# Four blocks of expert 0 moved into the end of the tile stage, and the adds made straight into the output

## The chip, the cores and the metric

The kernel runs on one core of one Trainium2 chip. The metric is the device time of the program in microseconds (us). Engines are called TensorE (PE in rows; PEld is its weight load), VectorE (DVE), ScalarE (ACT), GpSimd (POOL) and SyncE (SP, which here only issues transfers and waits). A "q" behind an engine's name means its queue.

## The reference

Cross attention of 2 x 1024 tokens of width 256 to 77 context rows with 16 heads, and then a feed-forward layer that is a mixture of 8 experts, of which each token uses the two with the highest logits:

```python
x = x + xattn(layernorm(x), ctx, ctx, mask, Wq, bq, Wk, bk, Wv, bv, Wo, bo)
x = x + ffn(layernorm(x), ln1_g, ln1_b, attn_w, ln2_g, ln2_b, gate_w, gate_proj, up_proj, down_proj)

def ffn(x, ...):
    h = x + (layernorm(x) * ln1_g + ln1_b) @ attn_w.T
    t = layernorm(h) * ln2_g + ln2_b
    logits = t @ gate_w.T                                 # 2048 x 8
    top_vals, top_idx = top_k(logits, 2)
    rw = softmax(top_vals)
    for e in range(8):
        g, u = t @ gate_proj[e].T, t @ up_proj[e].T       # 256 -> 1024
        out += comb[:, e:e+1] * ((silu(g) * u) @ down_proj[e].T)   # 1024 -> 256
    return h + out
```

Everything is 32-bit float.

## The kernel before

**Tile stage.** The 2048 tokens are 16 tiles of 128, batch 0 and 1 in turn. A software pipeline runs over them: in step `it` each engine does the stages LN1, XT, QK, PV, PROJ, LN2, MIX, LIST and SCATTER (lags 0 to 8) of the tiles it, it-1, ..., it-8. So steps 16 to 23 drain the pipeline, with fewer stages each. Each engine has its own instruction order, written out in a function `tiles(it)`; semaphores join them. On ScalarE step `it` ends with the exponentials of tile it-2 (`p_sb`, L646), and the next begins with `qT` (L611), which the score products (L1100) wait for. GpSimd computes the inverse roots of the norms (L495 to L498), scatters each tile's list entries (L517) and adds the residual (L523). SyncE stores each tile's normalized rows to `z2_rows` and its residual to `acc_rows` (`store`, L417).

LIST finds each token's two experts, and its place in each of their lists by two small products with the tokens before it (L1118, L1119). SCATTER writes (token, weight) into the lists in device memory, 2048 places for each expert.

**Seam.** When all tiles are listed, TensorE adds up the counts (L1162), and VectorE computes the tables on one partition (L910 to L956): how many blocks of 128 rows each expert has, which list row each block starts at (`row_tab`, released by `row_done`), which of three weight buffers it uses, and in which block the next expert's weights are to be split (`tab_done`). ScalarE, VectorE and GpSimd split expert 0's weights into a high and a low part there (L661, L656, L531, L966 to L968), since each expert product is made as three products of rounded pieces (L1168 to L1170).

**Expert stage.** A pipeline over 36 usual blocks (`USUAL_BLOCKS`; up to three more if present): GpSimd fetches the block's list (L553), gathers its rows (L560), TensorE transposes them (L1208, here called the block transposes), ScalarE and VectorE make the pieces `tb_hi` and `tb_lo`; TensorE computes gate and up in two halves (24 products of 512 columns in all, 6 for each half product), ScalarE silu, VectorE `act`; TensorE transposes act (L1199), the pieces `aT_hi` and `aT_lo` are made, then down is 24 products of 256 columns; VectorE weights the result (L979), GpSimd adds it to the rows in `acc_rows` by an accumulating indirect transfer (L570). SyncE loads the weights of experts 2 to 7 in four parts each (L439), as buffers come free. When all adds are in, SyncE copies `acc_rows` to the output (L447).

```python
            def experts_(it, only=None):                      # TensorE, L1182
                a, b, c = back(it, 0), back(it, 1), back(it, 2)
                # gate and up of b (half 0), act transposes of c, gate and up of b (half 1),
                # block transposes of a, down of c
```

## Time and profile before

| | us |
|---|---|
| median of 3 runs | 621.02 (617.53 to 622.01) |
| the profiled execution | 620.13 |
| its span | 618.6 |
| mean granted clock of TensorE | 0.932 of full speed |

The profile shows one execution, in microseconds from the start of its span. Busy time of an engine: TensorE 527.6 us (85%), VectorE 345.9 (56%), ScalarE 281.4 (45%), GpSimd 287.2 (46%). The granted clock is the share of TensorE's full clock that it was given. A timeline row gives start, length, engine, line, operation, output and inputs, and in brackets how long the engine had been idle before, and what released it. Several equal instructions in a row are merged (x2). The ends of matmuls are modelled: the pace is read from the distance of their starts.

### The profile page before, as it was taken

How to read it: one execution, taken by the hardware profiler on the slowest of the kernel's cores; microseconds unless marked ns; L12 is line 12 of the kernel's file. 1: busy time of each engine (PE TensorE's matmuls, PEld its weight loads, DVE VectorE, ACT ScalarE, POOL GpSimd, SP SyncE). 2: the span in 40 equal slices, each digit the busy share in tenths (PEclk: the TensorE clock that was granted, in tenths of full speed). 3: DMA queues.
4: the chain of work that ended last, by engine and by line, in shares of the span. 5: the costliest groups of instructions: out<-in, count | busy, mean ns of one | idle time of the engine just before them, and what ended most of it. 6: DMA issues, size and time to landing. Idle time of an engine off the chain costs nothing.

```text
span 618.6 us, 13662 instructions
## 1 busy us (share of the span) xinstructions
PE 527.6 (85%) x3197; PEld 452.7 (73%) x3198; DVE 345.9 (56%) x876; ACT 281.4 (45%) x701; POOL 287.2 (46%) x374
## 2 busy tenths in 40 slices
PE   2579999999997513899999998999999999999960
PEld 1357788888886302788888887888888888888850
DVE  1846788788876474466434345836536534365330
ACT  1177878787874141534323325434335323353210
POOL 4321436455545455357633416756554644345120
PEclk9779999999998555999999999899999999999995
DMA  8870010101010044011312375171262222612123
GB/s 217 217 314 0 19 36 18 35 17 34 17 35 27 27 86 161 10 28 27 44 26 34 77 211 178 17 200 55 43 187 59 34 43 28 179 55 34 17 23 143
DMA packets 27088, 46.57 MB, mean 75 GB/s; under 512 B 9718, under 2 KB 22544, under 8 KB 26768
## 3 DMA queue, kind: packets, MB, share of 16 engines
q1 hardware_dynamic: 15312, 35.77, 17.8%
q0 software_dynamic: 9088, 9.52, 9.7%
q10 hardware_dynamic: 2656, 0.91, 0.9%
q8 instruction: 13, 0.21, 0.2%
q14 instruction: 19, 0.16, 0.1%
HBM read 36.67 MB, written 11.61 MB: 78 GB/s over the span
## 4 chain that ended last, share of the span: by engine, by line
PE 65%; ACT 12%; DMA 7%; DVE 4%; issue 3%; POOL 1%; ACTq 0%; POOLq 0%; SPq 0%; DVEq 0%
PE psum L1168 15%; PE psum L1169 15%; PE psum L1170 15%; ACT p_sb L646 9%; PE psum L1100 6%; DMA w_raw<-in_experts 6%; PE psum L1199 4%; PE psum L1048 4%; PE psum L1043 2%; PE psum L1208 1%; ACT qT L611 1%; ACT uT L635 1%; PE psum L1055 1%; ACT rows L640 1%; PE psum L1064 1%
## 5 line engine op out<-in xcount | busy, mean ns | idle before, releaser
L1168 PE MATMUL psum<-w_hi,tb_hi 128*128 x288 | 117.9, 409 | 5.1 <-DVE tb_lo L1004 4.2
L1169 PE MATMUL psum<-w_lo,tb_hi 128*128 x288 | 113.7, 395 | 0.0
L1170 PE MATMUL psum<-w_hi,tb_lo 128*128 x288 | 113.7, 395 | 0.0
L1168 PE MATMUL psum<-w_hi,aT_hi 128*128 x288 | 85.0, 295 | 4.3 <-DVE aT_lo L992 4.3
L1169 PE MATMUL psum<-w_lo,aT_hi 128*128 x288 | 82.1, 285 | 0.0
L1170 PE MATMUL psum<-w_hi,aT_lo 128*128 x288 | 82.1, 285 | 0.0
L992 DVE TENSOR_TENSOR aT_lo<-psum,aT_hi 128x512 fp32r<-128x512 f32 x72 | 46.4, 685 | 63.0 <-ACT aT_hi L678 63.0
L674 ACT ACTIVATE silu<-psum 128x512 f32<-128x512 f32 x36 | 21.6, 600 | 117.4 <-PE psum L1170 117.4
L570 POOL DMA_INDIRECT acc_rows<-o_sb,add_at x36 | 58.6, 1629 | 34.1 <-POOL add_at L568 32.9
L998 DVE TENSOR_TENSOR act<-psum,silu 128x512 f32<-128x512 f32 x72 | 49.3, 686 | 33.8 <-PE psum L1170 28.5
L1168 PEld LDWEIGHTS psum<-w_hi,tb_hi 128*128 128x128 f32 x288 | 54.9, 191 | 16.9 <-issue 7.3
L646 ACT ACTIVATE p_sb<-s_sb,s_negmax 128x77 f32<-128x77 f32 x256 | 65.5, 348 | 1.1 <-DVE s_negmax L811 1.1
L560 POOL DMA_INDIRECT rows<-z_rows,gather_at x36 | 47.8, 1327 | 34.9 <-POOL gather_at L558 27.0
L1170 PEld LDWEIGHTS psum<-w_hi,tb_lo 128*128 128x128 f32 x288 | 54.7, 190 | 12.0
L1169 PEld LDWEIGHTS psum<-w_lo,tb_hi 128*128 128x128 f32 x288 | 54.9, 191 | 9.3
L1168 PEld LDWEIGHTS psum<-w_hi,aT_hi 128*128 128x128 f32 x288 | 55.6, 193 | 4.8 <-issue 4.8
L678 ACT ACTIVATE aT_hi<-psum 128x512 fp32r<-128x512 f32 x72 | 39.1, 595 | 43.6 <-PE psum L1199 43.6
L1169 PEld LDWEIGHTS psum<-w_lo,aT_hi 128*128 128x128 f32 x288 | 55.9, 194 | 0.0
L1170 PEld LDWEIGHTS psum<-w_hi,aT_lo 128*128 128x128 f32 x288 | 55.8, 194 | 0.0
L373 POOL TENSOR_TENSOR w_lo<-w_raw,w_hi (+1 forms) x8 | 34.6, 4325 | 45.2 <-DVE w_hi L988 45.2
L979 DVE TENSOR_SCALAR o_sb<-psum,blk 128x256 f32<-128x256 f32 x36 | 17.4, 482 | 65.8 <-PE psum L1170 30.6
L496 POOL TENSOR_SCALAR var_eps<-mv 128x1 f32<-128x1 f32 x48 | 11.6, 241 | 89.6 <-DVE mv L713 48.2
(170 smaller groups left out, 1029.5 us busy)
## 6 DMA issues: line engine op xcount, KB each, us to landing
w_raw<-in_experts SPq DMA_DIRECT2D x24, 768.0 KB, 4.4
w_raw<-in_experts SPq DMA_DIRECT2D x2, 3072.0 KB, 14.0
x_sb<-in_x SPq DMA_DIRECT2D x8, 256.0 KB, 5.8
z_rows<-rows SPq DMA_DIRECT2D x16, 128.0 KB, 1.7
acc_rows<-x_sb SPq DMA_DIRECT2D x16, 128.0 KB
ceil_f<-in_mask ACTq DMA_DIRECT2D x2, 308.0 KB, 11.6
blk<-lists POOLq DMA_DIRECT2D x36, 1.0 KB
rows<-z_rows,gather_at POOLq DMA_INDIRECT x36, 2.9
```

Source lines behind the costliest of these rows:

```text
L373: return engine.tensor_tensor(weights(w_lo, slot, at, cols), weights(w_raw, slot, at, cols), weights(w_hi, slot, at, cols).bitcast(F32), A ...
L560: nc.gpsimd.indirect_dma_start(zg[:, b[1], :], None, z2_rows, bass.IndirectOffsetOnAxis(ap=gather_at[:, b[1], :], axis=0), bounds_check=TO ...
L570: nc.gpsimd.indirect_dma_start(acc_rows, bass.IndirectOffsetOnAxis(ap=add_at[:, c.par, :], axis=0), y[:, c.par, :], None, bounds_check=TOK ...
L646: last = nc.scalar.activation(p_sb[:, t2[1], h * KEYS:(h + 1) * KEYS], s_sb[:, t2[1], h * KEYS:(h + 1) * KEYS], ACT.Exp, bias=s_negmax[:, ...
L678: nc.scalar.activation(aT_hi[:, c.par, 4 * half:4 * half + 4, :], bank[4 + half], ACT.Copy).then_inc(aTh_done, 1)
L992: nc.vector.tensor_tensor(aT_lo[:, c.par, 4 * half:4 * half + 4, :], bank[4 + half].rearrange("p (i t) -> p i t", i=4), aT_hi[:, c.par, 4 ...
L998: nc.vector.tensor_tensor(act[:, b.par, half * 512:half * 512 + 512], bank[1 + 2 * half], silu[:, half, :], ALU.mult).then_inc(act_done, 1)
L1048: done = nc.tensor.matmul(dst, rows_T[:, k, :], w[:, k, :], start=k == 0, stop=k == KD - 1)
L1100: last = nc.tensor.matmul(bank[g][:, (h0 - g * BANK_HEADS) * KEYS:(h1 - g * BANK_HEADS) * KEYS], qT[:, par, m, :], k_diag[:, par, m, h0 - ...
L1168: nc.tensor.matmul(dst, hi, weights(w_hi, slot, at, cols), start=first, stop=False)
L1169: nc.tensor.matmul(dst, hi, weights(w_lo, slot, at, cols), start=False, stop=False)
L1170: return nc.tensor.matmul(dst, lo, weights(w_hi, slot, at, cols), start=False, stop=last)
```

## The change

Rows 0 to 511 of expert 0's list are known once the first nine tiles are listed (if those tiles give at least 512; else the rest is left as padding and later tokens start at row 512). The change does these four blocks early, and starts the tables' count for expert 0 at row 512:

- SyncE fetches their list rows after tile 10's store. GpSimd waits in step 17 for them, for the stores, and for the last exponentials (the gathered rows, `ze`, lie over `p_sb`), and gathers block 0; blocks 1, 2 and 3 follow in steps 18, 20 and 21.
- Expert 0's weights are split in the tile stage: a quarter on ScalarE in steps 4 to 7, its low part on VectorE in steps 5 to 8. The buffers of the tile stage are laid out anew for that.
- The work of blocks 0 and 1 is written into steps 18 to 21 of TensorE, ScalarE and VectorE; the rest of block 1, and blocks 2 and 3, are written between VectorE's table operations. The late blocks follow as before, 32 of them, with their tables from index 0.
- Expert 1's split is fixed to block 3, and expert 2's load waits for the transposes of block 5.
- From tile 13 on GpSimd computes the router's exponential, as a power of e, instead of ScalarE.
- Rank products of the tiles behind 11 go to another bank of PSUM.
- `acc_rows` is the output itself, so rows are in the output's order (batch first), and the copy at the end is gone. All of `z2_rows` is filled with zeros in the prologue.

```diff
+EARLY, EARLY_TILES = 4, 9
+LIST_ROWS = EARLY * P + EXPERTS * TOKENS + SPARE * P
...
-        acc_rows = nc.dram_tensor("acc_rows", (TOKENS + P, D), F32).ap()
+        acc_rows = out
...
-            sp.dma_start(z2_rows[TOKENS:TOKENS + P, :], zeros[:, :]).then_inc(pad_out, 16)
+            sp.dma_start(z2_rows.rearrange("(c p) d -> p c d", p=P), zeros[:, :].unsqueeze(1).to_broadcast([P, TILES + 1, D])).then_inc(pad_out, 16)
...
-            pipeline(sp, store, TILES, 0, 0)
+            sp.wait_ge(pad_out, 32)
+            pipeline(sp, store, EARLY_TILES + 1, 0, 0)
+            store(Step((EARLY_TILES + 1) // 2, (EARLY_TILES + 1) % 2, 2))
+
+            for par in range(2):
+                sp.wait_ge(listed[par], 16 * TOPK * len(range(par, EARLY_TILES, 2)))
+            for j in range(EARLY):
+                sp.dma_start(blk[:, j], lists[j * P:(j + 1) * P, :]).then_inc(blk_early, 16)
+            for t in range(EARLY_TILES + 2, TILES):
+                store(Step(t // 2, t % 2, 2))
 
...
                 if e == 2:
                     sp.wait_ge(acc_out, 16 * TILES)
+                    sp.wait_ge(tb_ps, EARLY + 2)
...
             sp.wait_ge(added, every)
-            for b in range(BATCH):
-                sp.dma_start(out_tiles[:, b], acc_tiles[:, b]).then_inc(out_done, 16)
-            sp.wait_ge(out_done, 16 * BATCH)
+            sp.sem_inc(out_done, 1)
...
+                if within(t7, TILES) and isinstance(number(t7), int) and number(t7) >= SILU_TILES:
+
+                    pool.wait_ge(gap_done, number(t7) + 1)
+                    nc.gpsimd.tensor_tensor(e2[:, t7[1], :], base_e[:, :], gap[:, t7[1], :], ALU.pow).then_inc(e2p_done, 1)
...
+                if at_step(it, 17):
+                    for par in range(2):
+                        pool.wait_ge(z2_out[par], 16 * len(range(par, EARLY_TILES, 2)))
+                    pool.wait_ge(pad_out, 32)
+                    pool.wait_ge(p_done, PT_ROUNDS * TILES)
+                    pool.wait_ge(blk_early, 16 * EARLY)
+                    nc.gpsimd.tensor_copy(gather_at[:, :, :], blk[:, 0:EARLY, 0:1]).then_inc(ate_done, 1)
+                    wait_apart(pool, ate_done, 1, pool_met)
+                    gather_early(0)
+                if at_step(it, 18):
+                    gather_early(1)
+                if at_step(it, 20):
+                    gather_early(2)
+                if at_step(it, 21):
+                    gather_early(3)
+
...
+                if isinstance(number(it), int) and 4 <= number(it) < 8:
+
+                    at, cols = split_columns(number(it) - 4)
+                    act_e.wait_ge(w_in[0], 16)
+                    nc.scalar.activation(weights(w_hi, 0, at, cols), weights(w_raw, 0, at, cols), ACT.Copy).then_inc(hi_first, 1)
+
+                if at_step(it, 18):
+                    tb_out(block_(0))
+                if at_step(it, 19):
+                    tb_out(block_(1))
+                    silu_out(block_(0), 0)
+                    silu_out(block_(0), 1)
+                if at_step(it, 20):
+                    aT_out(block_(0), 0)
+                    silu_out(block_(1), 0)
+                if at_step(it, 21):
+                    aT_out(block_(0), 1)
...
+                if isinstance(number(it), int) and 5 <= number(it) < 9:
+
+                    at, cols = split_columns(number(it) - 5)
+                    dve.wait_ge(hi_first, number(it) - 4)
+                    nc.vector.tensor_tensor(weights(w_lo, 0, at, cols), weights(w_raw, 0, at, cols),
+                                            weights(w_hi, 0, at, cols).bitcast(F32), ALU.subtract).then_inc(lo_first, 1)
+
+                if at_step(it, 19):
+                    tb_pieces(block_(0))
+                if at_step(it, 20):
+                    act_out(block_(0), 0)
+                    act_out(block_(0), 1)
+                    tb_pieces(block_(1))
+                if at_step(it, 21):
+                    aT_rest(block_(0), 0)
+                    aT_rest(block_(0), 1)
+                    act_out(block_(1), 0)
...
-            step(nc.vector.tensor_copy(cnt[:, :], bank[0][0:1, 0:EXPERTS]))
+            step(nc.vector.tensor_tensor(cnt[:, :], bank[0][0:1, 0:EXPERTS], taken[:, :], ALU.add))
+            tb_pieces(block_(2))
+            weighted(block_(0))
...
-            step(nc.vector.tensor_scalar(row_tab[:, :], r_of[:, :], float(P), None, ALU.mult))
+            step(nc.vector.tensor_scalar(row_tab[:, :], r_of[:, :], float(P), float(EARLY * P), ALU.mult, ALU.add))
             dve.sem_inc(row_done, 1)
+
+            act_out(block_(1), 1)
+            for half in range(2):
+                aT_rest(block_(1), half)
+            act_out(block_(2), 0)
...
+            act_out(block_(2), 1)
+            tb_pieces(block_(3))
...
-            down_leftovers(nc.vector, dve, 0, 1, GU_COLS, DN_COLS // 2)
-            leftovers(0, 1, 0)
-            leftovers(0, 1, 1)
...
+                if at_step(it, 20):
+                    up_(block_(0), 1)
+                if at_step(it, 21):
+                    aT_(block_(0), 1)
...
+                if at_step(it, 18):
+                    tb_(block_(0))
+                if at_step(it, 19):
+                    pe.wait_ge(place_done, 13)
+                    tb_(block_(1))
+                    gate_(block_(0), 0)
+                    up_(block_(0), 0)
+                    gate_(block_(0), 1)
+                if at_step(it, 20):
+                    aT_(block_(0), 0)
+                    gate_(block_(1), 0)
+                    up_(block_(1), 0)
+                if at_step(it, 21):
+                    down_(block_(0), 0)
...
+            down_(block_(0), 1)
+            tb_(block_(2))
+            gate_(block_(1), 1)
+            up_(block_(1), 1)
...
+            for i in range(EARLY - 1, EARLY + 1):
+                experts_(block_(i))
+            pe.wait_ge(tab_done, 1)
+            pipeline(pe, experts_, USUAL_BLOCKS, 2, 2 * GATHERS, GATHERS, EARLY + 1)
```

## Rows read from the trace of the kernel before

**Rows 1.** page, forty slices of the span: TensorE's granted clock, in tenths

```profile
PEclk9779999999998555999999999899999999999995
```

**Rows 2.** table of stretches: stretch, length, busy us by engine, clock, DMA share, GB/s

```profile
60.00:120.00 60.00, 57.33 (x390) 48.64 (x389) 47.75 (x175) 49.22 (x168) 28.44 (x55) 1.00 0.08 25
210.00:240.00 30.00, 4.92 (x19) 3.38 (x19) 20.30 (x73) 7.18 (x9) 15.37 (x17) 0.50 0.43 100
```

**Rows 3.** timeline of TensorE: drain, seam, block transposes of blocks 0, 4, 35

```profile
202.65 2.08 PE L1048 MATMUL psum<-aw,uT 128*128 128x256 f32 x4 [0.24 <-ACT uT L635]
...
220.41 0.19 PE L1118 MATMUL psum<-chosen,below 128*128 128x8 bf16 x1 [1.58 <-DVE chosen L788]
...
240.38 0.66 PE L1208 MATMUL psum<-ident,rows 128*128 128x128 f32 x2 [19.51 <-DMA rows<-z_rows,gather_at]
...
278.92 0.38 PE L1208 MATMUL psum<-ident,rows 128*128 128x128 f32 x2
...
580.75 0.38 PE L1208 MATMUL psum<-ident,rows 128*128 128x128 f32 x2
```

**Rows 4.** timeline, end of the span: last add, then the output copy

```profile
600.54 1.58 POOL L570 DMA_INDIRECT acc_rows<-o_sb,add_at  x1 [1.21 <-issue]
605.58 1.62 SPq L447 DMA_DIRECT2D out_x<-acc_rows  x2
```

**Rows 5.** timeline of ScalarE: last exponentials; conversion of weights

```profile
184.19 4.10 ACT L646 ACTIVATE p_sb<-s_sb,s_negmax 128x77 f32<-128x77 f32 x16
...
223.90 3.69 ACT L656 ACTIVATE w_hi<-w_raw 128x2048 fp32r<-128x2048 f32 x2
```

**Rows 6.** chain that ended last, tile stage: start, us, what

```profile
165.88 2.84 ACT p_sb L646 x11
168.72 0.52 ACT qT L611 x2
```

**Rows 7.** timeline of GpSimd: tile 13's root, last scatter, first list fetch

```profile
185.97 0.19 POOL L495 TENSOR_SCALAR var_eps<-mv 128x1 f32<-128x1 f32 x1 [3.91 <-DVE mv L713]
...
223.54 1.18 POOL L517 DMA_INDIRECT lists<-pair,pos  x1 [0.30 <-issue]
...
231.02 0.62 POOL L553 DMA_DIRECT2D blk<-lists  x1 [3.92 <-issue]
```

**Rows 8.** page, DMA issues: out<-in, count, size, median us to landing

```profile
w_raw<-in_experts SPq DMA_DIRECT2D x24, 768.0 KB, 4.4
...
rows<-z_rows,gather_at POOLq DMA_INDIRECT x36, 2.9
```

**Rows 9.** page, costliest groups: VectorE's act operations, busy, mean ns of one

```profile
L998 DVE TENSOR_TENSOR act<-psum,silu 128x512 f32<-128x512 f32 x72 | 49.3, 686 | 33.8 <-PE psum L1170 28.5
```

**Rows 10.** timelines of VectorE and GpSimd: tables and leftover pass

```profile
221.48 0.28 DVE L912 TENSOR_TENSOR passed_n<-cnt,over 1x128 f32<-1x128 f32 x1
...
224.92 2.25 DVE L925 SCALAR_TENSOR_TENSOR r_of<-e_of,steps 1x40 f32<-1x40 f32 x1
...
227.42 0.17 DVE L927 TENSOR_SCALAR row_tab<-r_of 1x40 int32<-1x40 f32 x1
...
224.75 2.36 POOL L373 TENSOR_TENSOR w_lo<-w_raw,w_hi 128x1024 fp32r<-128x1024 f32 x1
```

**Rows 11.** timeline of TensorE: products and act transposes behind the seam

```profile
243.02 0.79 PE L1168 MATMUL psum<-w_hi,tb_hi 128*128 x1 [1.98 <-DVE tb_lo L1004]
...
246.59 0.63 PE L1170 MATMUL psum<-w_hi,tb_lo 128*128 x1
247.02 0.63 PE L1168 MATMUL psum<-w_hi,tb_hi 128*128 x1
...
248.24 0.40 PE L1168 MATMUL psum<-w_hi,tb_hi 128*128 x1
248.48 0.40 PE L1169 MATMUL psum<-w_lo,tb_hi 128*128 x1
...
256.23 1.04 PE L1199 MATMUL psum<-ident,act 128*128 128x128 f32 x8
```

More of the change, by code:

```diff
@@ L667, in experts_ @@
                 has = member(only)
-                if has(c):
+                if has(c) and not early(c):
                     splits = entry(act_e, splits_tab, c, 0, 1)
@@ new lines, in up_, with aT_ @@
+            def up_(b, half, slot=0):
+                n = number(b)
+                if early(b) and n == 0 and half == 1:
+                    pe.wait_ge(pT_done, PT_ROUNDS * TILES)
+                if early(b) and n == 1 and half == 1:
+                    pe.wait_ge(topi_done, TILES)
+                wait_count(pe, act_done, 2 * n - 1 + half)
+                half_product(b, slot, half, 1).then_inc(u_ps, 1)
+            def aT_(c, half):
+                n = number(c)
+                pe.wait_ge(act_done, 2 * n + half + 1)
+                if early(c) and n == 0 and half == 0:
+                    pe.wait_ge(act_done, 2)
+                if early(c) and n == 0 and half == 1:
+                    pe.wait_ge(x1_done, TILES)
+                if early(c) and n == 1 and half == 1:
+                    pe.wait_ge(y_done, 1)
+                wait_count(pe, aTl_done, 2 * n - 1 + half)
+                for i in range(4):
+                    at = half * 512 + i * P
+                    last = nc.tensor.transpose(bank[aT_bank(c, half)][:, i * P:(i + 1) * P], act[:, c.par, at:at + P], ident[:, :])
+                last.then_inc(aT_ps, 1)
@@ new lines, in tb_ @@
+            def tb_(a):
+                n = number(a)
+                if early(a) and n == 0:
+                    pe.wait_ge(q_done, KD * TILES)
+                if early(a) and n == 2:
+                    pe.wait_ge(place_done, TILES)
+                pe.wait_ge(zg_in[a[1]], 16 * (a[0] + 1))
+                wait_count(pe, tb_done, 2 * n)
+                for k in range(KD):
+                    last = nc.tensor.transpose(bank[6][:, k * P:(k + 1) * P], gathered(a)[:, k * P:(k + 1) * P], ident[:, :])
+                last.then_inc(tb_ps, 1)
@@ new lines, in down_ @@
+            def down_(c, half, slot=0):
+                n = number(c)
+                if half == 0:
+                    if early(c) and n == 0:
+                        pe.wait_ge(h_done, TILES)
+                    if early(c) and n == 1:
+                        pe.wait_ge(aTl_done, 2)
+                    wait_count(pe, y_done, n)
+                for i in range(half * IC // 2, (half + 1) * IC // 2):
+                    if i % 4 == 0:
+                        pe.wait_ge(aTl_done, 2 * n + i // 4 + 1)
+                    last = three_products(bank[y_bank(c)][:, 0:D], aT_hi[:, c.par, i, :], aT_lo[:, c.par, i, :], slot,
+                                          GU_COLS + i * D, D, i == 0, i == IC - 1)
+                if half == 1:
+                    last.then_inc(y_ps, 1)
```

345 lines of the change are left out of this document (217 added, 128 removed).

## The prediction

> **What bounds the kernel now.** I read the granted clock in the page's forty slices first [rows 1]: full nearly everywhere, but behind a third of the span it falls to its lower level (0.5 of full speed, 1.2 GHz). The table of stretches says what TensorE does there [rows 2]: in the tile stage it is busy 57.33 of 60 us, from 210 to 240 us only 4.92 of 30. The TensorE timeline of the seam [rows 3] says what the hole is. The last tile's rank product starts at 220.41. The next work is the first block's transpose at 240.38, after 19.51 us of waiting for the gathered rows; in between VectorE builds the tables and GpSimd fetches lists and rows. From then on the pace is TensorE's own: the block transposes (one pair for each of 36 blocks) start at 278.92 for block 4 and at 580.75 for block 35, 301.83/31 = 9.74 us a block. After the last block an add and then a copy of the whole output remain [rows 4]: the last add is issued at 600.54, the copy at 605.58, and the span ends at 618.6. So there are three costs to look at: the hole, 36 blocks, 13.0 us of copy.
>
> **Does the early work replace other work, or come on top?** A block is 128 list rows. From the reference's inputs I counted the routing: expert 0 gets 1279 rows, 749 of them in the first nine tiles (512 are needed), and all experts together need 36 blocks. With 512 rows of expert 0 taken off, 767 are left, 6 blocks instead of 10. So 4 early + 32 later = 36: no padding and no additional block.
>
> **Removed: the output copy.** From 605.58 to the span's end at 618.6: **-13.0 us** [rows 4]. The adds now go into the output itself; each was an add in device memory before too, so I price them alike.
>
> **Added in the tile stage.** ScalarE converts expert 0's weights in four pieces of 1536 columns at steps 4 to 7. Two pieces of 2048 took 3.69 us [rows 5], 1.84 each; three quarters, with a small fixed part, is 1.43 us. What would hide it? The chain of work in the tile stage [rows 6] goes from the exponentials on ScalarE to qT on ScalarE at once (168.72), and from there to the score products. The piece stands between the exponentials and qT, so nothing hides it: 4 x 1.43 = **+5.7 us** (0 if the chain has slack that the rows don't show). VectorE's four leftover pieces come at steps 5 to 8. No row of mine has VectorE at this; ScalarE's pace would make it 1.4 us, GpSimd's (2.36 us for 1024 columns, [rows 10]) 3.5; I take 1.7, nearer the faster one, as VectorE's act operations on 512 columns take 0.69 even out of PSUM [rows 9]. VectorE is busy 47.75 of 60 us in the tile stage [rows 2], which leaves 2 us of each step (about 10.3 us), and three of the four following steps are themselves longer by 1.43. I take these pieces at 0, up to 1.7 each if that cover is gone. The list base has one more small operation and a wait on VectorE in the prologue: +0.3. The zero fill writes seventeen copies of 128 KB instead of one, ahead of the first two experts' 6 MB. It lies beside the tiles' compute, since the first weights are wanted only at step 4; 0, up to 1 us on the loads issued just before it. Sum: S = **+6.0**.
>
> **The drain, step by step** (times as in the profile before, S left out). GpSimd at step 17 now waits for the last exponentials, which end at 184.19 + 4.10 = 188.29 [rows 5], because the gather's target lies over their buffer. Then a small copy, about 1.2 us to the indirect issue, and 1.1 us to issue. Queued behind this is the inverse root of tile 13, which ran at 185.97 [rows 7] and now starts near 190.7: **+4.7**. VectorE's z and o_sb wait for it, and TensorE behind them. I add 0.5 for TensorE's slower clock after that idle: +5.2. Gathered rows land 2.9 us after issue [rows 8], near 192.5, before step 18's end, so the gather itself is hidden.
> Step 19's last product on TensorE ended at 202.65 + 2.08 = 204.7 [rows 3]; now 209.9. Products of 512 columns follow each other every 0.43 us at the lower clock and every 0.23 to 0.24 at the higher [rows 11]. A half gate or up product is 6 of them: 2.6 or 1.4 us. The 8 act transposes of a block take 1.0 [rows 11]. What is left of a block's 9.74 us after four half products (5.6) and the transposes (1.0, 0.2) is the down product, 2.9.
> - Transposes of block 1 (0.4), one half product at the lower clock (2.6), two at the higher (2.8): 215.7.
> - Step 20 took about 4.6 of the 15.7 us from step 19's end to the last rank product [rows 3]; now with a half product (1.4) but mostly at the higher clock, which halves the rest: 3.6, to 219.3.
> - Transposes of act and two half products (3.3) to 222.6, just when the next tile's chosen experts come (some 3.4 us after step 20's last product, again out of those 15.7).
> - VectorE now has three block operations of 0.69 us [rows 9] before the last tile's maximum; the last rank product starts at about 227.25 instead of 220.41: **+6.85**.
> - Pair, count, pieces of block 2 and the weighting of block 0: the tables' second operation starts at 231.25 (was 221.48). From it to the end of the row table was 227.59 - 221.48 = 6.1 us. But one operation of 40 elements took 2.25 us beside GpSimd's 2.36 us leftover pass [rows 10]; the next operation of the same size, the row table's own, takes 0.17 to 0.19, and that pass is gone: 4.05, to 235.3.
> - Meanwhile TensorE does the rest of block 1 and half of block 2 and waits for act of block 1, which VectorE makes behind the row table: 236.05.
> - Transposes, two half products, block 3's transposes, down of block 1: 6.4, to 242.4. Four half products of block 3 (5.6) and act transposes (1.0): block 4's transposes start at **249.0**.
> They started at 278.92: **-29.9 us**. Four blocks at 9.74 are 39.0 us; 9 us of it are lost in the seam. The last list scatter ends near 232; before, the first list fetch came 7.5 us after the last scatter's issue (223.54 to 231.02) [rows 7], beside expert 2's weights. Even with that delay block 4's rows are there near 247, so the gather isn't the bound, by 2 us. Expert 2's load now starts only with block 5's transposes, but is wanted three blocks later (29 us) and its four parts of 4.4 us take 18 [rows 8]: hidden. Behind block 4 all switches of experts fall on the same block numbers as before, so 31 blocks and the end cost what they cost.
> **Where clock and page speak against it.** In the seam the clock fell after the idle time and came back only after about 5 us of dense products (243.0 to 248.2) [rows 11]. The new seam has work in small bursts with waits between. I add **+2.5** for one more stretch at the lower clock.
> The Trainium skill, page "TensorE: Matmul & The Clock Gate", section "HAM oscillation — how this bites in real kernels", says that short bursts of matmuls between waits throttle TensorE again each time, so the bursts keep running at half clock. The trace agrees so far as the clock fell in the drain; whether bursts of 3 to 6 us do it no row shows. It is the first rival below.
>
> **Sum** against the profiled execution's 620.1 us: 620.1 - 13.0 - 29.9 + 6.0 + 2.5 = 585.7, so **586 us**. That execution lies 0.9 under the median of 621.0, less than I can resolve.
>
> **Rivals.**
> 1. *The clock stays at the lower level in the bursts.* For: the clock of 0.5 from 210 to 240 us [rows 1, 2]. Against: from 210 us on TensorE would be dense. Price: the half products on the path to block 4, about 12 that I took at the higher clock, at 1.2 us more each, plus down (2.9) and transposes (some 2): +19. In place of my 2.5: 586 + 17 = **603 us**. If only up to the row table: 594.
> 2. *The tile stage absorbs the pieces, or the GpSimd wait is shorter.* ScalarE was busy 49.22 of 60 us of that stage [rows 2], so a wait could close. Then up to 5.7 + 2.5 less: **578 us**. Against: the chain, where each link follows the other at once [rows 6].
> 3. *Slower than before: the adds into the output set the pace.* An add took 605.4 - 600.54 = 4.9 us from issue to landing, and each next add waits for it; with 1.4 us of preparation it fits in 9.74 us. If adds into the output buffer took over 8.3 us, every microsecond more would cost 36. Slower than 627 us needs 627 - 586 = 41 us, so 9.5 us an add. Against: the copy wrote 2 MB there in 13 us without trouble [rows 4]. **630 us** at 9.6.
> 4. *The change doesn't do what it says*: were block 2 or 3's act held by the tables, early blocks would wait as the first block did, and only the copy and a part would be won: 620.1 - 13.0 + 6.0 = **613 us**.
>
> **How the numbers follow.** Forecast 0.70; rival 1 0.14 (0.06 of it at 600 or more); rival 2 0.09 (0.03 under 577); rival 3 0.02; rival 4 0.05. Range 577 to 600: beyond it lie 0.06 + 0.03 + 0.02 + 0.05 and a few hundredths for what I overlooked. One per cent, about what a measurement here can tell from no change, is 6.2 us: faster 0.95, same 0.02, slower 0.03.
>
> **What would show it.** Right: the block transposes at equal spacing, block 4's starting near 249 + 6 + 2.5 = 257 us; no SyncE copy at the end; the tile steps 4 to 7 longer by 1.4 us; tile 13's inverse root on GpSimd right behind the first gather; the small table operation at 0.2 us. Wrong: a TensorE wait over 5 us in the table stage, the first later block waiting for its gathered rows, a wait at the switch to expert 2, adds over 8 us, or a clock of 0.5 through the early blocks.

## The result, and the profile after

| | before | after |
|---|---|---|
| median of 4 runs, us | 621.51 (617.53 to 622.77) | 588.82 (588.05 to 592.96) |
| profiled execution, us | 620.1 | 589.26 |
| its span, us | 618.6 | 587.7 |
| last exponentials of the tile stage end | 188.29 | 192.90 |
| block 4's transposes start | 278.92 | 255.27 |
| last add issued | 600.54 | 576.18 |

The changed kernel takes 0.9494 of the time before, with a 95% interval of 0.9441 to 0.9548. That is 32.7 us less. The forecast was 586 (577 to 600), so it held, 2.8 us too low. One of its terms, the output copy, was wrong by 6.5 us, though, and misses of the other terms hid about half of that. So the closeness is partly luck.

The seam first. This is the TensorE timeline of the kernel after, from the end of the tile stage to the first block after the tables. The columns are as in [rows 3].

```profile
197.63 0.69 PE L1241 MATMUL psum<-ident,o_sb 128*128 128x128 f32 x2 [4.51 <-DVE o_sb L900]
...
207.29 2.19 PE L1262 MATMUL psum<-v_chunks,pT 128*128 128x34 f32 x10
209.28 0.67 PE L1445 MATMUL psum<-ident,ze 128*128 128x128 f32 x2
...
216.45 1.13 PE L1246 MATMUL psum<-aw,uT 128*128 128x256 f32 x4 [0.49 <-ACT uT L734]
217.42 0.38 PE L1445 MATMUL psum<-ident,ze 128*128 128x128 f32 x2
217.56 0.48 PE L1383 MATMUL psum<-w_hi,tb_hi 128*128 128x512 f32 x1
...
233.12 0.18 PE L1322 MATMUL psum<-chosen,below 128*128 128x8 bf16 x1 [0.74 <-DVE chosen L924]
...
245.79 0.38 PE L1445 MATMUL psum<-ident,ze 128*128 128x128 f32 x2
255.27 0.38 PE L1445 MATMUL psum<-ident,rows 128*128 128x128 f32 x2
264.73 0.38 PE L1445 MATMUL psum<-ident,rows 128*128 128x128 f32 x2
```

The last tile's rank product (L1322) starts at 233.12. Behind it there is no longer a hole of 19.51 us [rows 3]: the early blocks' work runs on, and block 4's transposes, the first out of `rows` instead of `ze`, start at 255.27. The one long wait left is the first line, 4.51 us, and it ends with VectorE's o_sb. VectorE itself waited 4.93 us for a root from GpSimd (`rstd`) just before; its row, and then GpSimd's timeline:

```profile
196.82 0.41 DVE L859 TENSOR_SCALAR z<-x_sb,mv,rstd 128x256 f32<-128x256 f32 x1 [4.93 <-POOL rstd L567]
...
193.17 0.19 POOL L611 COPY gather_at<-blk 128x4 int32<-128x4 int32 x1 [6.42 <-ACT p_sb L745]
194.34 1.09 POOL L600 DMA_INDIRECT ze<-z_rows,gather_at  x1 [0.97 <-POOL gather_at L611]
195.50 0.18 POOL L564 TENSOR_SCALAR var_eps<-mv 128x1 f32<-128x1 f32 x1
...
237.43 0.97 POOL L590 DMA_INDIRECT lists<-pair,pos  x1 [0.30 <-issue]
242.76 0.61 POOL L650 DMA_DIRECT2D blk<-lists  x1 [4.36 <-issue]
```

GpSimd waits for the last exponentials (ACT p_sb), makes the gather's indices, issues the gather, and only then reaches tile 13's inverse root at 195.50. In the table of stretches of the same kernel (stretch, length, busy us of PE, PEld, DVE, ACT and POOL with counts, granted clock, DMA share, GB/s) the clock is at its lower level right behind that wait and back at full from 220 us on:

```profile
190.00:200.00 10.00, 3.87 (x27) 2.92 (x26) 4.24 (x21) 4.33 (x16) 4.99 (x9) 0.75 0.08 24
200.00:210.00 10.00, 9.95 (x40) 8.73 (x38) 3.74 (x14) 2.00 (x6) 4.10 (x8) 0.50 0.23 29
210.00:220.00 10.00, 7.53 (x33) 5.99 (x34) 7.36 (x33) 5.02 (x12) 4.77 (x8) 0.72 0.09 28
220.00:230.00 10.00, 9.36 (x53) 7.35 (x51) 6.84 (x36) 4.58 (x11) 7.24 (x10) 1.00 0.20 54
230.00:260.00 30.00, 27.74 (x169) 24.27 (x170) 21.32 (x74) 8.16 (x16) 17.00 (x22) 1.00 0.17 32
```

Two small things that were to be seen are there. The table operation of 40 elements, 2.25 us in [rows 10], takes 0.19 us now:

```profile
240.96 0.19 DVE L1124 SCALAR_TENSOR_TENSOR r_of<-e_of,steps 1x40 f32<-1x40 f32 x1
```

And the end. This is the last add in the GpSimd timeline of the kernel after:

```profile
576.18 1.57 POOL L667 DMA_INDIRECT out_x<-o_sb,add_at  x1 [0.87 <-POOL add_at L665]
```

This is the view of its line 152, where each engine leaves the program (queue, operation, count: shortest, median and longest ns, first and last start):

```profile
L152 SPq DRAIN  x1: 7/7/7, 580.9 to 580.9; - x1
L152 POOLq DRAIN  x1: 5265/5265/5265, 581.7 to 581.7; - x1
L152 PEldq DRAIN  x1: 73/73/73, 587.4 to 587.4; - x1
```

And this, with the same columns, is the view of its line 393, the test of whether a block behind the usual ones is present:

```profile
L393 PEldq COMPARE_BRANCH  x7: 210/1381/2810, 574.0 to 584.7; - x7
```

A DRAIN is here the last thing that an engine does before the semaphores of the common end. SyncE is done at 580.9, 4.7 us behind the last add's issue, and that is where I had the end of the kernel. But GpSimd's DRAIN runs until 587.0, and TensorE's queue is busy until 587.4 with branches over seven absent blocks. From the last add's issue to the end of the span it is 11.5 us; the forecast had left 5.0 (605.58 - 600.54).

### The profile page after: what moved, and what is told of

It reads as the page before. It is cut to its first block, busy times and chain, and to the rows that moved or that the text cites. A ratio compares the mean times of both kernels' runs of the same rounds, so it can differ in the third digit from the quotient of the medians.

```text
span 587.7 us, 13275 instructions
## 1 busy us (share of the span) xinstructions
PE 523.3 (89%) x3198; PEld 450.5 (77%) x3199; DVE 345.3 (59%) x882; ACT 281.3 (48%) x699; POOL 283.1 (48%) x371
## 3 DMA queue, kind: packets, MB, share of 16 engines
q0 software_dynamic: 8960, 9.51, 10.2%
## 4 chain that ended last, share of the span: by engine, by line
PE 64%; ACT 13%; DVE 6%; DMA 5%; issue 4%; POOL 1%; SPq 0%; ACTq 0%; POOLq 0%; DVEq 0%
PE psum L1383 15%; PE psum L1384 14%; PE psum L1385 14%; ACT p_sb L745 9%; PE psum L1298 6%; DMA w_raw<-in_experts 4%; PE psum L1432 4%; PE psum L1246 4%; PE psum L1241 2%; ACT uT L734 1%; PE psum L1445 1%; ACT qT L710 1%; PE psum L1262 1%; PE psum L1253 1%; ACT rows L739 1%
## 5 line engine op out<-in xcount | busy, mean ns | idle before, releaser
L1383 PE MATMUL psum<-w_hi,tb_hi 128*128 (+1 forms) x288 | 116.8, 405 | 2.7 <-DVE tb_lo L1025 1.7
L1385 PE MATMUL psum<-w_hi,tb_lo 128*128 (+1 forms) x288 | 112.6, 391 | 0.0
L1384 PE MATMUL psum<-w_lo,tb_hi 128*128 (+1 forms) x288 | 112.6, 391 | 0.0
L779 ACT ACTIVATE silu<-psum 128x512 f32<-128x512 f32 x72 | 43.1, 599 | 132.7 <-PE psum L1385 124.9
L1383 PE MATMUL psum<-w_hi,aT_hi 128*128 (+1 forms) x288 | 84.6, 294 | 4.1 <-DVE aT_lo L1036 4.1
L1384 PE MATMUL psum<-w_lo,aT_hi 128*128 (+1 forms) x288 | 81.5, 283 | 0.0
L1385 PE MATMUL psum<-w_hi,aT_lo 128*128 (+1 forms) x288 | 81.4, 283 | 0.0
L667 POOL DMA_INDIRECT out_x<-o_sb,add_at x36 | 59.6, 1656 | 34.2 <-POOL add_at L665 31.8
L1383 PEld LDWEIGHTS psum<-w_hi,tb_hi 128*128 128x128 f32 x288 | 54.2, 188 | 13.3 <-issue 4.1
L1031 DVE TENSOR_TENSOR act<-psum,silu 128x512 f32<-128x512 f32 x72 | 49.4, 687 | 24.9 <-PE psum L1385 18.1
L657 POOL DMA_INDIRECT rows<-z_rows,gather_at x32 | 41.9, 1308 | 30.8 <-POOL gather_at L655 24.2
L1298 PE MATMUL psum<-k_diag,qT 128*128 128x308 f32 (+2 forms) x128 | 40.1, 459 | 15.2 <-ACT qT L710 9.8
L1043 DVE TENSOR_SCALAR o_sb<-psum,blk 128x256 f32<-128x256 f32 x36 | 17.4, 482 | 60.4 <-PE psum L1385 28.9
## 6 DMA issues: line engine op xcount, KB each, us to landing
ceil_f<-in_mask ACTq DMA_DIRECT2D x2, 308.0 KB, 11.5
```

What stands on the lines that cost most here:

```text
L657: nc.gpsimd.indirect_dma_start(zg[:, b[1], :], None, z2_rows, bass.IndirectOffsetOnAxis(ap=gather_at[:, b[1], :], axis=0), bounds_check=TO ...
L667: nc.gpsimd.indirect_dma_start(acc_rows, bass.IndirectOffsetOnAxis(ap=add_at[:, c.par, :], axis=0), y[:, c.par, :], None, bounds_check=TOK ...
L779: nc.scalar.activation(silu[:, half, :], bank[half_banks(b, half)[0]], ACT.Silu).then_inc(silu_done, 1)
L1031: nc.vector.tensor_tensor(act[:, b.par, half * 512:half * 512 + 512], bank[half_banks(b, half)[1]], silu[:, half, :], ALU.mult).then_inc(a ...
L1298: last = nc.tensor.matmul(bank[g][:, (h0 - g * BANK_HEADS) * KEYS:(h1 - g * BANK_HEADS) * KEYS], qT[:, par, m, :], k_diag[:, par, m, h0 - ...
L1383: nc.tensor.matmul(dst, hi, weights(w_hi, slot, at, cols), start=first, stop=False)
```

## The experiments

The question for the end: is the time behind the last add that of the engines' own closing work, which the copy had covered? For the tile stage: what do the pieces cost, and on which engine? For the drain: what do GpSimd's wait and the clock cost? Each kernel below is the changed one with one edit, unless it says otherwise; each ratio is to runs of the kernel before that were taken beside it (medians 618.8 to 621.7). "Not to be told apart by the times" means that the 95% intervals of two ratios overlap widely; the profiles show one execution each.

**Copy put back** (accumulate in a buffer of its own, copy at the end):

```
-        acc_rows = out
+        acc_rows = nc.dram_tensor("acc_rows", (TOKENS + P, D), F32).ap()
...
-            sp.sem_inc(out_done, 1)
+            for b in range(BATCH):
+                sp.dma_start(out[b * SEQ:(b + 1) * SEQ, :], acc_rows[b * SEQ:(b + 1) * SEQ, :]).then_inc(out_done, 16)
+            sp.wait_ge(out_done, 16 * BATCH)
```

> The changed kernel with its own accumulation buffer and the output copy put back at the end; all else as changed. Theory A (the copy used to cover the engines' own way to the end of the program, 6.6 us of it): the copy takes 13.0 us from its issue, which again lies 4.9 us behind the last add's issue, so the span ends 17.9 us behind the last add's issue instead of 11.5, and the time is 6.4 us longer, 595.2 us. Theory B (the copy's 13.0 us were all gained, and the 6.6 us that are missing lie elsewhere, in slower adds into the output): 13.0 longer, 601.8 us, or if the adds become quicker again, something between; the distance from the last add's issue to the copy's issue would then be well under 4.9 us.

Measured 593.3 (592.27 to 595.81), ratio 0.9548 (0.9514 to 0.9581): about 4.5 us more than the changed kernel, not 13. The copy, now of contiguous rows, is issued at 584.30, and SyncE's DRAIN is at 592.9, so this copy took 8.6 us where the one before took 12.7 (605.58 to 618.3). And it isn't what ends the profiled execution of 594.2 us; TensorE's DRAIN is, behind branches of up to 5.06 us beside the copy:

```profile
L152 PEldq DRAIN  x1: 73/73/73, 593.9 to 593.9; - x1
```

Why those branches were longer, and whether the order of the rows made the copy shorter, isn't shown. So this run alone doesn't price the old copy. The next one does.

**The kernel before without its copy** (list and rows in batch order, so that the sums can go into the output):

```
-        acc_rows = nc.dram_tensor("acc_rows", (TOKENS + P, D), F32).ap()
+        acc_rows = out
...
-            for b in range(BATCH):
-                sp.dma_start(out_tiles[:, b], acc_tiles[:, b]).then_inc(out_done, 16)
-            sp.wait_ge(out_done, 16 * BATCH)
+            sp.sem_inc(out_done, 1)
```

> The kernel before with only this part of the change: the adds go straight into the output, rows in the output's order, no copy at the end. My prediction's term was -13.0 us: 608.5 us. Theory A: in the kernel before TensorE's queue was done at 601.9 us and GpSimd's drain at 610.1, against the span's end at 618.6, so only 8 to 8.5 us are gained: 613.2 us; with a drain as long as in the changed kernel (5.3 us from 602.5) up to 10.8: 610.7. Theory B (slow adds into the output): under 7 us gained, and adds longer than before.

Measured 612.72 (610.22 to 614.29), ratio 0.9852 (0.9813 to 0.9892), so 9.0 us less than the 621.69 beside it, clear of noise (the interval gives 7 to 12). Its last add is issued at 603.98 and the span ends at 612.6, 8.6 us behind. This is its GpSimd's closing DRAIN:

```profile
L140 POOLq DRAIN  x1: 6497/6497/6497, 605.9 to 605.9; - x1
```

and this the same in the kernel before, under the copy of [rows 4]:

```profile
L140 POOLq DRAIN  x1: 7635/7635/7635, 602.5 to 602.5; - x1
```

Without a copy the span ends with GpSimd (605.9 + 6.5 = 612.4). In the kernel before GpSimd was busy until 610.1 and nobody saw it, as the copy ran to 618.3. So at most 8 or 9 us could be won there.

**Three tests instead of seven at the end**, and **tests nested**, so that the first absent block skips all others:

```
-            for j in range(USUAL_BLOCKS, EARLY + BLOCKS):
+            for j in range(USUAL_BLOCKS, BLOCKS):
```
```
-            for j in range(USUAL_BLOCKS, EARLY + BLOCKS):
+            def behind(j):
+                if j == EARLY + BLOCKS:
+                    return
                 with eng.If(eng.value_load(present_tab[0:1, j - EARLY:j - EARLY + 1], min_val=0, max_val=1)):
...
+                    behind(j + 1)
+            behind(USUAL_BLOCKS)
```

> The changed kernel with three tests for absent blocks at the end instead of seven (of what is computed nothing changes for these inputs; lists of more than 39 blocks would lose some). Theory A1 (TensorE's queue, which walks over the seven absent blocks until 587.4 us, ends the program): TensorE is done near 580, and GpSimd's drain, which ended at 587.0 in the changed kernel, becomes the end; GpSimd has four tests of 0.78 us less ahead of its drain, so between 0.4 and 3.5 us faster, I take 2.5: 586.3 us. Theory A2 (GpSimd's drain ends a fixed time, about 9.2 us, behind the last add's issue whatever stands ahead of it): 0.4 us faster, 588.4. Theory B (slow adds): no change.

> The changed kernel with the tests for absent blocks nested, each inside the one before, so that one test is made when no block is present and the code of all seven is jumped over at once; nothing is left out. Theory A1: as with three tests or a little better, 585 to 586.5 us. Theory A2: 588.4. If a far jump costs as much as several near ones (the branches of TensorE took 0.2 to 2.8 us each), then not better than three tests.

Three tests: 588.18 (586.03 to 590.59), ratio 0.9484 (0.9439 to 0.9529), not to be told apart from the changed kernel by the times. In the profile the last add to the end of the span is 9.5 us, where it was 11.5. Nested: 585.57 (584.06 to 588.46), ratio 0.9441 (0.9396 to 0.9486), 3.2 us less by the medians with intervals that still overlap, and 9.2 us from the last add to the end. The closing of both queues in the nested kernel:

```profile
L152 PEldq DRAIN  x1: 73/73/73, 575.1 to 575.1; - x1
...
L152 POOLq DRAIN  x1: 5897/5897/5897, 576.9 to 576.9; - x1
```

TensorE is through 1.3 us behind the issue of the last add (573.82), where it was 11.2 in the kernel after, and GpSimd's DRAIN alone sets the end (576.9 + 5.9 = 582.8, of 583.0). One branch of 3.36 us is left on TensorE, and it ends at 575.0, before GpSimd's DRAIN starts. GpSimd's tests cost less than their own length: in the seven kernels that make one or three of them its DRAIN takes 6.5 to 7.6 us where it starts about 2 us behind the last add's issue, and 5.8 to 5.9 where it starts about 3 behind, and it ends 8.4 to 9.6 behind; in the seven kernels with seven tests it takes 5.27 and ends 10.7 to 10.8 behind. In five of the kernels below that keep the seven tests the span ends 12.0 to 13.0 us behind the last add, always with TensorE's DRAIN, while GpSimd's ends before: there TensorE's walk over the absent blocks decides.

**ScalarE's pieces twice**, each of the four written a second time by the same operation behind the first:

```
                     nc.scalar.activation(weights(w_hi, 0, at, cols), weights(w_raw, 0, at, cols), ACT.Copy).then_inc(hi_first, 1)
+                    act_e.wait_ge(hi_first, 2 * (number(it) - 4) + 1)
+                    nc.scalar.activation(weights(w_hi, 0, at, cols), weights(w_raw, 0, at, cols), ACT.Copy).then_inc(hi_first, 1)
```

> The changed kernel with each of ScalarE's four conversions of expert 0's weights (tile steps 4 to 7) made twice. Theory A (they stand on the chain from the exponentials to the score products, nothing covers them): a second time adds 4 x 1.4 to 1.5 us: 588.8 + 5.8 = 594.6 us, steps 4 to 7 are 13.1 us long. Rival B (part was covered by waits): under 3 us more.

Measured 602.69 (602.05 to 603.69), ratio 0.9724 (0.9677 to 0.977): 13.9 us more, over twice what was expected. The tile stage alone grew by 12.7 (here and below from the third tile's score products to the last exponentials). First the chain in the kernel after (ScalarE and TensorE timelines):

```profile
61.45 4.09 ACT L745 ACTIVATE p_sb<-s_sb,s_negmax 128x77 f32<-128x77 f32 x16
65.44 1.48 ACT L753 ACTIVATE w_hi<-w_raw 128x1536 fp32r<-128x1536 f32 x1
66.82 0.61 ACT L710 ACTIVATE qT<-psum,bq_scaled 128x128 f32<-128x128 f32 x2
...
67.48 2.34 PE L1298 MATMUL psum<-k_diag,qT 128*128 128x462 f32 x8 [1.72 <-ACT qT L710]
```

then a step of the doubled one:

```profile
67.70 1.47 ACT L753 ACTIVATE w_hi<-w_raw 128x1536 fp32r<-128x1536 f32 x1
69.20 1.48 ACT L755 ACTIVATE w_hi<-w_raw 128x1536 fp32r<-128x1536 f32 x1
70.59 0.61 ACT L710 ACTIVATE qT<-psum,bq_scaled 128x128 f32<-128x128 f32 x2
...
71.25 4.47 PE L1300 MATMUL psum<-k_diag,qT 128*128 128x462 f32 x8 [3.24 <-ACT qT L710]
```

and two stretches of its tile stage:

```profile
60.00:90.00 30.00, 23.07 (x126) 18.48 (x125) 19.06 (x46) 22.09 (x59) 7.06 (x16) 0.83 0.05 18
90.00:120.00 30.00, 26.41 (x162) 21.63 (x162) 23.54 (x76) 22.33 (x67) 11.61 (x20) 0.88 0.06 19
```

The piece lies between exponentials and qT, as forecast, and each copy adds 1.4 to 1.5 us to TensorE's wait (0.35 without a piece, 1.72 with one, 3.24 with two). The rest goes with the clock: in the changed kernel it was 1.00 in these stretches, and here it is 0.83 and 0.88. From these mean clocks some 17 of the 60 us ran at the lower level, an estimate, which can cost up to 8.7 us; 6.8 were to be explained. The same eight score products take 4.47 us instead of 2.34 when the clock has fallen in that wait. The longer wait isn't needed for it: the profiled execution with the copy put back has the same in a milder form, though its tile stage and its waits of 1.72 us are those of the changed kernel: score products of 4.02 us, two steps of 13.3 us, 3.2 us more in the stage.

**VectorE's work twice** (one more pass of 1536 columns ahead of each leftover):

```
                     dve.wait_ge(hi_first, number(it) - 4)
+                    nc.vector.tensor_tensor(weights(w_hi, 0, at, cols), weights(w_hi, 0, at, cols).bitcast(F32),
+                                            weights(w_hi, 0, at, cols).bitcast(F32), ALU.max).then_inc(hi_again, 1)
+                    dve.wait_ge(hi_again, number(it) - 4)
```

> The changed kernel with one more VectorE pass of 1536 columns (a maximum of the high part with itself) ahead of each of its four leftover subtractions in tile steps 5 to 8. Theory A (VectorE waits 0.7 to 1.9 us a step for scores, which covered the first pass): the second, 1.7 us, exceeds what is left of that cover (0.73 to 1.6 us a step, and nothing in the step after the last): 3 to 5 us more, 592.8 us. Rival B (VectorE has still room, its pieces are free): under 1 us more. Rival C (its pieces weren't covered even once, so the second costs in full): 7 us more.

Measured 597.22 (595.21 to 599.12), ratio 0.9628 (0.9573 to 0.9684): 8.4 us more. In the profiles (8.9 us apart) the tile stage takes 4.2 of it, as theory A had it, the drain 2.6, the expert stage 0.7 and the end 1.4; the drain and the end have the same code in both kernels. In the drain the clock stays low longer than in the kernel after:

```profile
200.00:210.00 10.00, 7.01 (x29) 6.13 (x30) 5.04 (x22) 2.47 (x7) 6.78 (x11) 0.50 0.25 53
210.00:220.00 10.00, 7.98 (x31) 6.35 (x31) 6.28 (x27) 2.29 (x7) 3.63 (x5) 0.50 0.08 26
```

**Pieces on GpSimd instead of ScalarE** (same place in the steps 4 to 7):

```
-                    act_e.wait_ge(w_in[0], 16)
-                    nc.scalar.activation(weights(w_hi, 0, at, cols), weights(w_raw, 0, at, cols), ACT.Copy).then_inc(hi_first, 1)
...
+                    pool.wait_ge(w_in[0], 16)
+                    nc.gpsimd.tensor_copy(weights(w_hi, 0, at, cols), weights(w_raw, 0, at, cols)).then_inc(hi_first, 1)
```

> The changed kernel, only the four early pieces of expert 0's rounded weights (1536 columns each, steps 4 to 7) are made by GpSimd in place of ScalarE. Theory A (the pieces cost what they take on ScalarE's chain from the exponentials to qT, 4.8 us measured at the end of the tile stage): the four steps go back from 11.6 to about 10.3 us, the score products from step 5 on start 1.3 us apart less, and the time falls by 4.8 us, 588.8 to 584. The rival (GpSimd's own chain, or a VectorE slowed beside a GpSimd pass as in the 2.25 us table operation of 40 elements): a pass of 1536 columns takes 3.5 us on GpSimd and stands ahead of the next inverse root, VectorE's operations beside it take longer, and the steps stay at 11.6 us or more: 589 or above.

Measured 587.26 (585.58 to 588.55), ratio 0.9481 (0.9424 to 0.9539), by the times not to be told apart from the changed kernel; the span is 3.1 us shorter. One piece on GpSimd, a step's score products, and VectorE's leftover, out of the timelines:

```profile
54.37 1.47 POOL L602 CAST w_hi<-w_raw 128x1536 fp32r<-128x1536 f32 x1
...
65.30 2.34 PE L1299 MATMUL psum<-k_diag,qT 128*128 128x462 f32 x8 [0.35 <-ACT qT L716]
...
70.25 1.75 DVE L1006 TENSOR_TENSOR w_lo<-w_raw,w_hi 128x1536 fp32r<-128x1536 f32 x1
```

The wait for qT is back at 0.35 us. From one step's score products to the next it takes 8.8, 10.3 and 10.3 us where the changed kernel took 10.2, 11.6 and 11.6. But then follow 11.9, 11.1 and 10.8, against 11.8, 10.3 and 10.7. The tile stage is 3.2 us shorter than in the changed kernel, not 4.8. In the changed kernel VectorE waited 0.75 and 0.73 us for scores in the two last steps with its pieces; here it doesn't wait for them, and TensorE waits for VectorE instead (0.72 and 0.78 us for `h`). So VectorE's pieces of 1.75 us had been free only because ScalarE's pieces made the steps longer.

**Gather 0 and its wait behind the inverse roots** (the wait for the exponentials moved from step 17 to step 18, behind that step's roots):

```
                 if at_step(it, 17):
...
-                    pool.wait_ge(p_done, PT_ROUNDS * TILES)
...
-                    gather_early(0)
+                if at_step(it, 18):
+                    pool.wait_ge(p_done, PT_ROUNDS * TILES)
+                    wait_apart(pool, ate_done, 1, pool_met)
+                    gather_early(0)
```

> The changed kernel with GpSimd's wait for the last exponentials and the gather of block 0 moved from the end of step 17 to step 18, behind the inverse roots of tiles 13 and 12. Theory A (the wait held the root of tile 13 back, and with it VectorE, TensorE and the clock): tile 13's root runs at once, TensorE's wait of 4.51 us for o_sb goes to about 0, part of step 18 runs at the higher clock again; block 0's rows land at the same time as before. 4.5 us, plus 1 to 3 for the clock: 588.8 - 6 = 582.8 us. Rival B (the drain absorbs it, because the later steps wait for other things, the tables and the burst of early block products): under 2 us gained, 587 to 589.

Measured 584.93 (582.52 to 588.93), ratio 0.9441 (0.9371 to 0.9511): 3.9 us less by the medians, with intervals that overlap, so the profile has to show it. TensorE's wait of 4.51 us at the head of step 18 is gone, and the clock is 1.00 from 180 to 200 us; it falls later (0.66 from 200 to 210, 0.82 from 210 to 220). From the last exponentials to block 4's transposes it takes 56.0 us, against 62.4 in the kernel after and 60.0 in the kernels with three and with nested tests, whose drain is the same code.

**Down part of expert 0 later** (pieces of 1024 columns; the third that the down product needs is converted at step 18 by ScalarE and left over at step 19 by VectorE):

```
-            return r * WCOLS // 4, WCOLS // 4
+            return r * GU_COLS // 4, GU_COLS // 4
...
+                    nc.scalar.activation(weights(w_hi, 0, GU_COLS, DN_COLS), weights(w_raw, 0, GU_COLS, DN_COLS), ACT.Copy).then_inc(hi_first, 1)
```

> The changed kernel, only the down part of expert 0's weights (a third) is taken out of the four pieces, which then have 1024 columns, and is converted by ScalarE at step 18 and left over by VectorE at step 19. Theory A (price is columns on ScalarE's chain): each piece 0.4 to 0.5 us shorter, together -1.7; in the drain the 2048 columns take 1.9 us on ScalarE at the time where TensorE waits for GpSimd's late inverse root anyway: 588.8 - 1.7 = 587.1. Rival (the drain's chain goes through ScalarE's b-tile outputs, which now stand behind it): +1.9 there, 589 in all.

Measured 590.18 (589.31 to 591.25), ratio 0.952 (0.9468 to 0.9572), not to be told apart from the changed kernel. The tile stage is 2.1 us shorter (1.7 expected). The drain takes 64.8 us in this execution, with the clock at 0.50 from 200 to 220 us; whether the moved pieces or the clock cost its 2.4 us more, this run can't tell.

**Combined.** Nested tests, gather later and down part later; then the same with the pieces on GpSimd; then that one without the down part's move.

> Three edits together on the changed kernel: the absent blocks' tests nested (alone it measured 585.6), the gather of block 0 behind the inverse roots, and only gate and up of expert 0 split in tile steps 4 to 8 (1024 columns a step instead of 1536), the down part on ScalarE at the end of step 18 and on VectorE in step 19, where both are idle. Theory A: -3.2 for the tests, -6 for the gather, 4 x 0.47 = -1.9 for ScalarE's shorter pieces: 588.8 - 11.1 = 577.7 us. If the gather's wait is absorbed (rival B of that run): 583.5. If the down part's pass on VectorE gets in the way of the drain: up to 2.3 us more.

> The combined kernel (nested tests of the absent blocks, gather 0 behind the inverse roots, down part later: 578.5) with the 1024-column pieces made by GpSimd in place of ScalarE. Theory A: the four steps of 11.2 go back to 10.3, 4 x 0.95 = 3.8 us less: 574.8. The rival (GpSimd's pass delays inverse roots or slows VectorE): no gain, 578 or above.

> The best combined kernel without its down part: nested tests of the absent blocks, gather 0 behind the inverse roots, the four pieces of 1536 columns on GpSimd, nothing of expert 0 left for the drain. Theory D (in the drain the later down part stands on the chain that the alone-standing run of it showed: 1.4 us slower than the changed kernel in spite of 2 us won in the tile stage, so 3.4 us lost there, while on GpSimd the shorter pieces win nothing): faster than the combined kernel of 575.9, near 573. The rival (the gains just add: 588.8 - 3.2 - 3.9 - 1.6 = 580.1, and the down part in the drain costs nothing once the gather stands behind the inverse roots): 580, slower than 575.9.

First: 578.54 (577.07 to 579.86), ratio 0.9338 (0.9288 to 0.9388). With the pieces on GpSimd: **575.93** (573.18 to 576.51), ratio 0.9281 (0.9224 to 0.9338). Without the down part's move: 579.61 (576.74 to 580.52), ratio 0.9339 (0.9288 to 0.939). My theory that the down part costs more in the drain than it saves fell: without the move the kernel isn't faster. The last two intervals overlap, so that the move gains something isn't shown either. From the last exponentials to block 4's transposes the three take 55.2, 55.2 and 55.9 us.

## Why the prediction held, step by step

Put against the profiled executions, the four stretches add up to the whole difference of the spans (618.6 - 587.7 = 30.9):

| stretch | forecast, us | measured, us |
|---|---|---|
| up to the last exponentials | +6.0 | +4.6 |
| from there to block 4's transposes | -27.4 | -28.3 |
| from there to the last add | 0 | -0.7 |
| from there to the end | -13.0 | -6.5 |
| sum | -34.4 | -30.9 |

**The end is the step that failed.** "From 605.58 to the span's end at 618.6: -13.0 us" took the copy's own time for what its removal gives. I had the kernel end where the last add lands. The stretch from the last add to the end was 18.1 us; in the kernel before without the copy it is 8.6. So the copy was worth 9.5 in the profile and 9.0 by the times; the other 4 us of its 13 were cover for GpSimd's DRAIN. The change also raises the number of tests behind the last usual block from three to seven, and I had priced nothing for them. They took 2 to 3 us more: 11.5 against 9.5 with three tests in the changed kernel, and 8.6 in the one before without its copy. What would have told me was in the trace of the kernel before: the DRAIN of 7.6 us at 602.5 and the branches.

**The tile stage.** Counted from the third score product, to leave out a prologue that came out 1.2 us shorter, the last exponentials come 5.8 us later. (In the profiles of the twelve kernels with the change these products start at 45.6 to 47.2 us, in the two without it at 46.8 and 47.6, so the 1.2 us lie within the scatter of single executions.) The forecast of the pieces was right: four pieces at 1.43 us gave 5.7. A piece took 1.48, in the very place that [rows 6] led to. VectorE's piece took 1.75 where I chose 1.7 between 1.4 and 3.5, and the case "up to 1.7 each if that cover is gone" shows in the kernel with the pieces on GpSimd, whose tile stage is still 2.7 us longer than that of the kernel before, 0.7 a piece. That the cover was for the most part ScalarE's own lengthening, I had only half seen.

**The drain.** Without my 2.5 us for the clock I had 249.0 - 188.29 = 60.7 us from the last exponentials to block 4; measured were 62.4 in the kernel after and 60.0 in two runs of the same code. The wait on GpSimd is right to 0.2 us (tile 13's root at 195.50 - 4.61 = 190.9, forecast 190.7). What I had too small is the clock behind it: steps 18 and 19 ran at the lower level, and step 19's last product ended (216.45 + 1.13) 24.7 us after the last exponentials instead of 21.6. I had put 0.5 us there, and 2.5 in general. The half products behind it ran at the higher clock from the first, where I had counted one at the lower, which gave 1.6 back. The 4.65 us from the act transposes at 222.6 to the last rank product at 227.25 had no full working. The last rank product came 40.2 us after the exponentials instead of 39.0, the row table's end (241.57) 48.7 instead of 47.0, and block 4 at 255.27, where the prediction said near 257.

**The clock, rival 1.** It did fall behind the 4.51 us wait, and stretches of 0.50 and 0.72 followed. Then it came back and stayed at 1.00 from 220 us on, across waits of up to 1.3 us between its bursts, so the 17 us of that rival didn't come. The Trainium skill, page "TensorE: Matmul & The Clock Gate", section "HAM oscillation — how this bites in real kernels", has bursts throttled again by each DMA wait between them. This trace agrees for the one long wait, here for VectorE and not for a DMA, and gives no sign of it for the short ones. How much a fall costs changes from run to run: the same drain took 60.0 to 60.4 us in five profiles, 62.4 in the changed kernel's, and 65.0 in that with VectorE's work twice, where the clock was 0.50 over the whole of 200 to 220 us. Why it returns earlier in one run than in another, these runs don't settle.

**The other rivals.** Rival 2: the tile stage absorbed nothing of ScalarE's pieces. Rival 3: adds into the output cost nothing; 31 blocks from block 4 to block 35 take 556.73 - 255.27 = 301.5 us, before 301.83. (No row shows the landing at 605.4 that rival 3 was worked out from; SyncE, which waits for it, issued the copy at 605.58.) Rival 4: TensorE waited 1.34 us for the act of block 1, which VectorE makes behind the row table (241.80 behind 241.57), and no early block waited longer. **A small miss:** GpSimd idles for 4.36 us again ahead of the first list fetch, at 242.76, while no weights are being loaded (expert 2's load starts at 265.19). So the weights aren't needed for the delay that I had put down to them. The code has a wait there that I had left out: ahead of this fetch GpSimd waits until all scatters have landed (`listed`), and in the kernel before a scatter landed 2.4 to 7.0 us behind its issue, 3.3 in the median. That is about the size of the idle time, an argument and not a test; that the fetch came 5.3 us behind the last scatter's issue instead of 7.5 fits with GpSimd's leftover pass of 2.36 us, which stood between them before. It did not delay block 4.

## What to carry to other kernels

Before a last transfer is priced at its own length, read what each engine does until the end below it: the gain is the distance to the next one that finishes. Code for blocks that are usually absent isn't free at the end of a program; nest the tests so that the first absent one skips the rest, and don't expect more than the next engine's end allows (GpSimd's DRAIN here). A piece put into a wait-free chain costs its time there, and TensorE's clock can fall in the longer wait, and then it costs about twice that (12.7 us for 5.9); a wait for a transfer's target belongs behind the small operations that others wait for.

## What the hardware showed that I had not expected

- Branches on TensorE's queue over absent blocks took 0.21 to 2.81 us each in the changed kernel, 1.38 in the median, beside 0.045 us on ScalarE's and GpSimd's and 0.056 on VectorE's for the same seven tests. Beside the copy that was put back they took up to 5.06 us, and the one branch over all seven nested blocks 3.36. Why TensorE's are so long, no run here tests. The Trainium skill, page "Advanced Engine Details and Errata", section "Control Flow Timing", gives about 108 ns for a compare-and-branch; TensorE's here are 13 times that in the median, and the other engines' about half of it.
- GpSimd's closing DRAIN, behind the last indirect add, took 5.3 to 7.6 us in all fourteen profiles of this study; where the kernel keeps seven tests it took 5.27 every time.
- GpSimd converts 128x1536 fp32 values in 1.47 us, as fast as ScalarE (1.48); its leftover pass, which has two operands, took 2.36 us for 1024 columns [rows 10].
- Adding 5.9 us of ScalarE work to the tile stage lengthened it by 12.7, with TensorE's clock down to 0.83 and 0.88 over 60 us of it: eight score products took 4.47 us instead of 2.34.
